# A state-space scan on one core: the inputs of every second unit come from ScalarE and TensorE, and most products with C run on GpSimd

## What is computed

```python
xz = einsum('bld,ed->ble', x, W_in);  xp, z = split(xz, 2)
xc = silu(conv_b + causal_conv(xp, conv_w))             # 512 channels
dbc = einsum('ble,fe->blf', xc, W_x)                    # dt | B (16) | C (16)
delta = softplus(einsum('blr,er->ble', dt, W_dt) + b_dt)
dA  = exp(delta[..., None] * A)                         # 512 channels x 16 states
dBx = delta[..., None] * Bm[:, :, None, :] * xc[..., None]
h_t = dA_t * h_{t-1} + dBx_t                            # scan over 256 tokens
y = einsum('bles,bls->ble', hs, Cm) + xc * Dp
y = y * silu(z);  x = layernorm(x + einsum('ble,de->bld', y, W_out))
# then attention and experts: x = layernorm(x + ffn(x))
```

## Time and profile before

| | us |
|---|---|
| median of 3 runs | 837.95 (837.55 to 838.26) |
| the profiled execution | 834.06 |
| its span, first to last instruction | 832.3 |
| VectorE busy from 70 to 283 us, the scan | 205.84 of 213 |
| GpSimd busy there | 189.78 |
| TensorE busy there | 173.34 |
| ScalarE busy there | 128.25 |

### The profile page before, as it was taken

The page is one execution under the profiler, slowest core; times in us unless marked ns, Lnnn a source line. Parts: engine busy times, 40 slices in busy tenths (PEclk is TensorE's granted clock), DMA queues, the critical chain, the costliest instruction groups (busy, mean ns, idle before and its releaser), DMA issues.

```text
span 832.3 us, 12019 instructions
## 1 busy us (share of the span) xinstructions
PE 753.3 (91%) x3991; PEld 566.9 (68%) x4000; DVE 611.8 (74%) x1243; ACT 452.8 (54%) x957; POOL 327.2 (39%) x183
## 2 busy tenths in 40 slices
PE   6985787788868999999999999998899999999996
PEld 2431233334434588898889898997777889898986
DVE  2688999999998877766884877577657373737376
ACT  3696656667546267755772766476544151515151
POOL 9007999898877832111110121112315030303030
PEclk9996999999999999999999999998989999999999
DMA  8000000000000200100000011011305552525201
GB/s 292 26 1 1 0 1 0 0 0 1 0 1 0 102 1 26 52 26 27 27 26 26 25 38 38 2 39 58 96 1 124 151 150 72 150 70 153 68 0 50
DMA packets 14458, 39.98 MB, mean 48 GB/s; under 512 B 2368, under 2 KB 3904, under 8 KB 14288
## 3 DMA queue, kind: packets, MB, share of 16 engines
q1 hardware_dynamic: 14416, 39.46, 15.5%
HBM read 38.34 MB, written 1.11 MB: 47 GB/s over the span
## 4 chain that ended last, share of the span: by engine, by line
PE 52%; DVE 18%; issue 14%; ACT 11%; POOL 3%; DMA 1%; DVEq 0%; SPq 0%; ACTq 0%; POOLq 0%
PE ps L872 13%; PE ps L874 12%; PE ps L873 12%; PE ps L439 6%; DVE m_ring L749 4%; POOL m_ring L326 2%; ACT a_p L1148 2%; PE ps L370 2%; PE ps L994 2%; DVE m_ring L754 2%; ACT a_vh L1140 2%; PE ps L397 2%; DVE a_p L1248 2%; DVE e_aw L1733 1%; PE ps L443 1%
## 5 line engine op out<-in xcount | busy, mean ns | idle before, releaser
L326 POOL TENSOR_TENSOR m_ring<-m_du,m_b_sb 128x1024 f32<-128x1024 f32 x64 | 149.6, 2358 | 66.9 <-DVE m_du L722 46.3
L749 DVE TENSOR_TENSOR_SCAN m_ring<-ps,m_ring 128x1024 f32<-128x1024 f32 x64 | 145.5, 2283 | 4.6 <-POOL m_ring L326 2.8
L950 POOL TENSOR_TENSOR a_wl<-raw,a_wh 128x1024 fp32r<-128x1024 f32 x16 | 40.0, 2498 | 236.3 <-ACT a_wh L1136 236.3
L439 PE MATMUL ps<-m_ring,ident 128*128 128x512 f32 x256 | 128.8, 618 | 0.1
L1464 POOL TENSOR_TENSOR e_wl<-raw,e_wh 128x512 fp32r<-128x512 f32 (+1 forms) x55 | 58.2, 1067 | 138.8 <-ACT e_wh L1575 74.7
L618 ACT ACTIVATE ps<-m_delta,m_negA 128x510 f32<-128x510 f32 x128 | 82.7, 682 | 6.2 <-DVE m_ring L749 4.2
L439 PEld LDWEIGHTS ps<-m_ring,ident 128*128 128x128 f32 x256 | 50.6, 198 | 44.0 <-issue 41.3
L872 PE MATMUL ps<-a_rowsh,e_wh 128*128 128x512 f32 x200 | 79.6, 398 | 0.7 <-DVE e_aw L1725 0.7
L873 PE MATMUL ps<-a_rowsl,e_wh 128*128 128x512 f32 x200 | 78.9, 395 | 0.0
L874 PE MATMUL ps<-a_rowsh,e_wl 128*128 128x512 f32 x200 | 78.8, 394 | 0.0
L569 ACT ACTIVATE m_b_sb<-ps 128x512 f32<-128x512 f32 x64 | 38.0, 594 | 64.3 <-PE ps L383 61.3
(11 more groups left out here) (202 smaller groups left out, 2067.7 us busy)
## 6 DMA issues: line engine op xcount, KB each, us to landing
raw<-in_expert_w SPq DMA_DIRECT2D x30, 384.0 KB, 3.5
raw<-in_attn_w SPq DMA_DIRECT2D x20, 512.0 KB, 3.3
e_wb<-wt SPq DMA_DIRECT2D x20, 256.0 KB, 4.7
e_wb<-wt SPq DMA_DIRECT2D x4, 448.0 KB, 6.3
e_wb<-wt SPq DMA_DIRECT2D x4, 384.0 KB, 4.5
e_wb<-wt SPq DMA_DIRECT2D x4, 320.0 KB, 4.5
m_first<-in_xT SPq DMA_DIRECT2D x2, 512.0 KB, 5.2
x<-in_x_tok SPq DMA_DIRECT2D x1, 1024.0 KB, 10.6
```

Of the source, the lines that this page charges most:

```text
L326: nc.gpsimd.tensor_tensor(split(slot(n)), du[:, pair_of(ph):pair_of(ph) + 2, halves(ph)], b_sb[:, n % B_BUFS:n % B_BUFS + 1, :].to_broadca ...
L439: nc.tensor.matmul(ps[:, Y_BANK + c, :], ident[:, :], slot(n)[:, c * HALF:(c + 1) * HALF], start=False, stop=False, skip_group_check=True) ...
L749: nc.vector.tensor_tensor_scan(slot(n), dA_of(n), slot(n), 0.0, ALU.mult, ALU.add).then_inc(scan_done, 1)
L950: nc.gpsimd.tensor_tensor(w[1][:, j, :], raw[:, j, :], w[0][:, j, :].bitcast(F32), ALU.subtract).then_inc(w_done, 1)
```

## The change

Units are now handled in pairs, an even one and an odd one.

- **Even units** get their input from GpSimd as before (`unit_in`), but the spread B comes by DMA: rows B and C (fp32) are written to DRAM once, and SyncE loads each row into all 128 partitions (`load_b`), three buffers.
- **Odd units** get their input from ScalarE: `du` is turned once for each chunk and half so that tokens lie on partitions (`turn_du`, `take_du`); B is turned too (`turn_b`, `take_b`), so that it is a scale for each partition; four activations of 128x256 make the product (`product`), and TensorE turns it back into PSUM with eight transposes (`turn_in`), where the scan reads it.
- **Decays**: those of even units stay in PSUM (one buffer of two banks), those of odd units go to SBUF (`decay_of`, two buffers). The other two banks hold the turned input of the odd unit.
- **Products with C**: VectorE makes 25 of the 64, those for which `by_vector` holds, with C spread by TensorE; GpSimd makes 39, with C spread by DMA (`load_c`), three buffers. `broadcast_b`, `copy_b` and `copy_c` are gone.
- Sums into y are added two units later, all in one order, and `pack`, the statistics and the rows of the norm move by some units.

```diff
-B_BUFS = 4
-B_AHEAD = 5
-BY_POOL = UNITS // 4 - 1
+B_BUFS = C_BUFS = 3
...
+TURN_AT = (4, 6, 18, 20, 22, 24)
 
 
 OUT_AT = (36, 44, 52, 56)
 
...
+    DA_BANK, IN_BANK, Y_BANK, TURN_BANK, C_BANK = 4, 6, 2, 0, 1
+
+    def decay_of(n):
+        if n % 2 == 0:
+            return banks(ps, DA_BANK, 2)
+        k = n // 2 % 2
+        if n < UNITS // 2:
+            return wh[:, k * UNIT:(k + 1) * UNIT]
+        return wl[:, (2 + k) * UNIT:(3 + k) * UNIT]
+
+    def du_T(half, i):
+
+        at = (2 - 2 * half) * UNIT + i * E_IN
+        return wl[:, at:at + E_IN]
+
+    PROD_MOVES = UNITS // 2 + 4
+
+    def prod_of(n, i):
+
+
+        k = n // 2 % 2
+        if n < PROD_MOVES:
+            at = (2 + k) * UNIT + i * 2 * P
+            return wh[:, at:at + 2 * P]
+        return delta[:, 2 * k + i // 2, i % 2 * 2 * P:(i % 2 + 1) * 2 * P]
 
...
-        return n - min((n + 3) // 4, BY_POOL)
+        return n % NS % 3 == 1 or n % NS == NS - 1 or n == UNITS - 2
+
+    def vector_below(n):
+        return sum(by_vector(m) for m in range(n))
+
+    def pool_below(n):
+        return n - vector_below(n)
 
...
+        def load_b(n):
+            k = n // 2
+            if k >= B_BUFS:
+                sp.wait_ge(dbx_ready, k - B_BUFS + 1)
+            sp.dma_start(b_sb[:, k % B_BUFS, :], bc_dram[n % NS:n % NS + 1, halves(phase(n))].to_broadcast([P, HALF])
+                         ).then_inc(ld_b[k % B_BUFS], 16)
+
+        def load_c(n):
+            k = pool_below(n)
+            if k >= C_BUFS:
+                sp.wait_ge(hcp_ready, k - C_BUFS + 1)
+            row = NS + n % NS
+            sp.dma_start(c_sb[:, k % C_BUFS, :], bc_dram[row:row + 1, halves(phase(n))].to_broadcast([P, HALF])
+                         ).then_inc(ld_c[k % C_BUFS], 16)
+
+        sp.wait_ge(rows_ready, 1)
+        sp.dma_start(bc_dram, bc_rows).then_inc(rows_stored, 16)
+        sp.wait_ge(rows_stored, 16)
+        load_b(0)
+        load_b(2)
+        load_c(0)
+        for n in range(0, UNITS, 2):
+            if n + 4 < UNITS:
+                load_b(n + 4)
+            for m in (n + 1, n + 2):
+                if m < UNITS and not by_vector(m):
+                    load_c(m)
+
...
-        for n in range(UNITS):
+        for n in range(0, UNITS, 2):
             unit_in(n)
-            if n >= 3 and by_pool(n - 3):
-                times_c(n - 3)
-
+            for m in (n - 3, n - 2):
+                if m >= 0 and not by_vector(m):
+                    times_c(m)
...
+        pool.wait_ge(prod_ready, UNITS // 2)
         for j in range(GH):
             pool.wait_ge(wh_done, j + 1)
+            if j >= 2:
+                pool.wait_ge(scan_done, UNITS - 6 + 2 * j)
...
         def broadcast_c(n):
-            if n and by_pool(n - 1):
-                pe.wait_ge(c_sb_ready, (n - 1) // 4 + 1)
-            nc.tensor.matmul(ps[:, C_BANK, :], sel[:, NS + n % NS, :], bcp[:, halves(phase(n))],
+            if n > 1:
+                pe.wait_ge(hc_ready, vector_below(n))
+            nc.tensor.matmul(ps[:, C_BANK, :], sel[:, n % NS, :], bcp[:, halves(phase(n))],
                              start=True, stop=True).then_inc(c_ready, 1)
+
+        def turn_b():
+
+            for i in range(TT):
+                mm = nc.tensor.transpose(ps[:, TURN_BANK, i * NS:(i + 1) * NS], bc_rows[0:NS, i * P:(i + 1) * P],
+                                         ident[0:NS, 0:NS])
+            mm.then_inc(turn_ready, 1)
+
+        def turn_du(k):
+
+            half, c = k // EC, k % EC
+            pe.wait_ge(turn_free, k + 1)
+            pe.wait_ge(du_ready, c + 1)
+            for i in range(TT // 2):
+                mm = nc.tensor.transpose(ps[:, TURN_BANK, i * P:(i + 1) * P],
+                                         du[:, c, (half * TT // 2 + i) * P:(half * TT // 2 + i + 1) * P], ident[:])
+            mm.then_inc(turn_ready, 1)
+
+        def turn_in(n):
+
+            pe.wait_ge(prod_ready, n // 2 + 1)
+            if n == 1:
+                pe.wait_ge(pair_free, 3 * EC)
+            else:
+                pe.wait_ge(scan_done, n - 1)
+            for c in range(2):
+                for i in range(TT // 2):
+                    mm = nc.tensor.transpose(ps[:, IN_BANK + c, i * P:(i + 1) * P], prod_of(n, i)[:, c * P:(c + 1) * P],
+                                             ident[:])
+            mm.then_inc(in_ready, 1)
 
...
+        def sum_unit(n):
             if n % NS == 0:
                 start_y(phase(n))
-            for back in (1, 2):
-                if n >= back and by_pool(n - back):
-                    pe.wait_ge(hcp_ready, (n - back) // 4 + 1)
-                    sum_y(n - back, back - 1)
-
-        for n in range(UNITS):
-            step(n)
-            if n == UNITS - 4:
-                pe.wait_ge(b_sb_ready, UNITS)
+            if by_vector(n):
+                pe.wait_ge(hc_ready, vector_below(n + 1))
+            else:
+                pe.wait_ge(hcp_ready, pool_below(n + 1))
+            for c in range(2):
+                sum_y(n, c)
+
+        for n in range(UNITS + 2):
+            if n in TURN_AT:
+                turn_du(2 + TURN_AT.index(n))
+            if n - 2 in vector_units[:-1]:
+                broadcast_c(vector_units[vector_units.index(n - 2) + 1])
+            if n == UNITS - 2:
+                pe.wait_ge(o_free, N_OUT)
                 rows.turn(pe, 0, 0)
-            if n == UNITS - 3:
+            if n == UNITS:
                 pe.wait_ge(scan_done, UNITS - 1)
                 rows.turn(pe, 0, 1)
-                pe.wait_ge(o_free, N_OUT)
                 first_parts(5)
+            if n >= 2:
+                sum_unit(n - 2)
+            if n % 2 and n + 2 < UNITS:
+                turn_in(n + 2)
+            if n - 1 in OUT_AT:
+                out_pair(OUT_AT.index(n - 1))
...
+        def take_b():
+            act.wait_ge(turn_ready, 1)
+            nc.scalar.activation(b_T.rearrange("p i s -> p (i s)"), ps[:, TURN_BANK, 0:TT * NS], ACT.Copy
+                                 ).then_inc(turn_free, 1)
+
+        def take_du(k):
+
+            half, c = k // EC, k % EC
+            act.wait_ge(turn_ready, k + 2)
+            if k == 0:
+                act.wait_ge(rows_stored, 16)
+            at = (2 - 2 * half) * UNIT
+            out = wl[:, at:at + 2 * UNIT].rearrange("p (i e) -> p i e", i=TT // 2)[:, :, c * P:(c + 1) * P]
+            nc.scalar.activation(out, ps[:, TURN_BANK, :].rearrange("p (i e) -> p i e", i=TT // 2), ACT.Copy
+                                 ).then_inc(turn_free, 1)
+
+        def product(n):
+
+            ph = phase(n)
             if n >= 4:
-                act.wait_ge(hcp_ready, n // 4)
-            nc.scalar.activation(c_sb, ps[:, C_BANK, :], ACT.Copy).then_inc(c_sb_ready, 1)
+                act.wait_ge(in_ready, n // 2 - 1)
+            if n % NS == 1:
+                act.wait_ge(turn_free, 1 + EC * (ph // 2) + pair_of(ph) + 2)
+            for i in range(TT // 2):
+                tile = ph // 2 * (TT // 2) + i
+                mm = nc.scalar.activation(prod_of(n, i), du_T(ph // 2, i)[:, pair_of(ph) * P:(pair_of(ph) + 2) * P],
+                                          ACT.Copy, scale=b_T[:, tile, n % NS:n % NS + 1])
+            mm.then_inc(prod_ready, 1)
 
...
         act.wait_ge(a_ready, 1)
-        act.wait_ge(dA_zeroed, 1)
-        for n in range(UNITS):
+        act.wait_ge(dA_zeroed, 2)
+        for n in range(0, UNITS, 2):
             decay(n)
-            if n >= 2 and by_pool(n - 2):
-                copy_c(n - 2)
-            if n - B_AHEAD + 1 in OUT_AT:
-                take_out(OUT_AT.index(n - B_AHEAD + 1))
-                copy_b(n + 1)
-            if n + 2 < UNITS and n - B_AHEAD + 2 not in OUT_AT:
-                copy_b(n + 2)
+            decay(n + 1)
+            if n + 3 < UNITS:
+                product(n + 3)
+            if n - 2 in TURN_AT:
+                take_du(2 + TURN_AT.index(n - 2))
+            if n - 4 in OUT_AT:
+                take_out(OUT_AT.index(n - 4))
             if n in PACK_AFTER:
                 pack(PACK_AFTER.index(n))
             if n == ROOTS_AFTER:
                 roots(0)
-            if n in SCALE_AFTER:
-                scale_row(SCALE_AFTER.index(n))
+            for i in range(TT // 2):
+                if n == SCALE_AFTER[i]:
+                    scale_row(i)
         act.wait_ge(keep["ld_ln1"], 16)
-        act.wait_ge(dbx_ready, UNITS)
+        act.wait_ge(dbx_ready, UNITS // 2)
...
         def scan(n):
             dve.wait_ge(dA_ready, n + 1)
-            dve.wait_ge(dbx_ready, n + 1)
-            nc.vector.tensor_tensor_scan(slot(n), dA_of(n), slot(n), 0.0, ALU.mult, ALU.add).then_inc(scan_done, 1)
+            if n % 2:
+                dve.wait_ge(in_ready, n // 2 + 1)
+                if n >= RING:
+                    dve.wait_ge(summed, 2 * (n - RING + 1))
+                unit_in = banks(ps, IN_BANK, 2)
+            else:
+                dve.wait_ge(dbx_ready, n // 2 + 1)
```

(2 more changed lines are left out.)

138 lines of the change are left out of this document (64 added, 74 removed).

## The result

The changed kernel takes **812.76 us** at the median (809.37 to 816.08 in four runs), against 837.75 for the kernel before on the same chip: a ratio of 0.9703 (95% interval 0.9669 to 0.9736), 25 us faster. The prediction was 815, range 804 to 832. The profiled execution of the changed kernel took 816.08 us, the longest of its four; they fall into two pairs, 815.65 and 816.08 at a mean granted clock of 0.968, and 809.37 and 809.88 at 0.978 and 0.982. The profiled execution of the kernel before (834.06, clock 0.974) is shorter than each of its four times here (836.95 to 838.26). So the two profiles, set side by side, show less than the whole gain.

The account below looks back on a forecast made before the run. VectorE's own instructions in the scan stage were taken to bound the kernel. 834.06 - 26.9 - 7.0 + 7.8 + 1.5 + 0.5 + 1.0 = 811.0, plus 3.9 for the median gives 815 us, range 804 to 832.

Parts of the forecast that it names:

- Products leaving VectorE, -26.9: Scan stage: VectorE makes 25 products with C instead of 49, so 24 at 1.12 us, 26.9 us, go.
- GpSimd 97% full: Scan stage: GpSimd's 18 instructions take 41.6 us of a 42.9 us phase; its work stays hidden with 1.3 us to spare.
- Scans of both forms, ScalarE's product, the loads: Scan stage: odd scans cost the same 2.19 us; a 128x256 activation takes 0.49 us; loads landing in 4.7 us stay hidden.
- The waits of before, -7.0: Scan stage: VectorE's earlier waits for spread C, GpSimd's input and decays inside the stage go, 7.0 us.
- The new wait behind output pairs, +7.8: Scan stage: VectorE waits for turned inputs queued behind four output pairs on TensorE, 2.7 us twice and 1.2 twice.
- the layout by hand: Scan stage: one phase laid out with the paces, timing GpSimd's products, TensorE's sums and turns against VectorE's need.
- The clock at the start, +1.5: Scan stage: low TensorE clock (0.50 from 70 to 76 us) makes some turns late by one or two us; 1.5 put.
- The stage, 190: From first scan to last product with C: 190 us instead of 213.
- Start +0.5, end +1.0: ScalarE's work before the first scan adds 0.5 us; TensorE's norm turns ahead of the last two sums add 1.0.
- A wait at most odd units: Scan stage: GpSimd and TensorE pass delays to turns, 0.5 us at 32 odd units, 16 us more: 829; chance 0.20.
- GpSimd falling behind: Scan stage: GpSimd's products wait 1.5 us each for DMA-loaded rows, 58 us: 868; chance 0.04 slower, 0.02 the same.
- The rule of the Trainium skill on transposes: TensorE in the stage: transposes don't count as clock activity like matmuls, pushing towards a low-clock slowdown; that case's chance 0.06.

Follow-up runs that it names:

- experiment 6: The changed kernel with four more products with C on GpSimd (43 instead of 39) and four fewer on VectorE (21 instead of 25): 816.19 us.
- experiment 3: The changed kernel with six added fp32 matmuls of 128x512, results unused, around TensorE's first turns at the start of the scan: 811.45 us.

## Why the prediction was right, and where it was not

- **Products leaving VectorE, -26.9.** 49 became 25 at 1.20 us each. Put back alone they brought 22.4 us of VectorE's work and 19.8 of stage. As terms of the same sum: VectorE's work fell by 25.3, which is 26.9 less the 2.6 by which short operations grew, and 1.0 more, half of it scans that are shorter by 8 ns (2.275 us for 2.283), the rest less overlap lost than the sum took off. That GpSimd's load would hold up VectorE's short operations was in no term.
- **GpSimd 97% full.** 71 operations at 2.36 us, but busy for 90% (170.7 of 189.5 us): it idled 18.9 us, nearly all of it waiting for scans. That it had no room for more was right (experiment 6), though not because it was full: what came too late was single products.
- **Scans of both forms, ScalarE's product, the loads.** 2.28 us for both, 0.494 for a taken 0.49, and 3.5 (C) and 4.0 us (B) to landing for a bound of 4.7. None of them made VectorE wait.
- **The waits of before, -7.0.** The sum took them all away. In their place are 1.9 us of small waits, which no term held.
- **The new wait behind output pairs, +7.8.** The mechanism was right, the size was not: 2.53 and 1.36 us at the first two, none and 0.53 with the last two, 4.4 in all for 2.7 + 2.7 + 1.2 + 1.2. The first was met in each part (pair, two sums, turn). At the second VectorE had one more product with C of its own to make meanwhile, which the layout by hand had left out.
- **The clock at the start, +1.5.** 2.7 us, in one piece at unit 5. The idle time is 4.4 + 2.7 + 1.9 = 9.0 for a predicted 9.3: that these errors (-3.4, +1.2, +1.9) cancel is luck.
- **The stage, 190.** It is 189.5. But the prediction's own terms for it, 212.8 - 26.9 - 7.0 + 7.8 + 1.5, give 188.2; its 190 counts the start and the end (+1.5) in, which lie outside the stage.
- **Start +0.5, end +1.0.** Measured -0.8 and +0.8. du was finished 0.9 us earlier than before, so GpSimd and ScalarE could begin sooner. Together they are 1.5 less than predicted, and the stage's gain is 1.3 less (23.3 for 24.6): the sum of -23.1 against a measured -23.3 is as close as it is because the two cancel.
- **The rivals.** A wait at most odd units did not come: there was none of over 0.3 us at 28 of the 32. GpSimd falling behind needs more work than the change gave it, and no load was late. The mean clock of the stage was 0.96. The rule of the Trainium skill on transposes, which would have brought it down, is not borne out at this mix of turns and matmuls; where the clock did fall (70 to 80 us, and 100 to 105 in experiment 3) TensorE had been idle for part of the time ahead.
- **A slip that changes nothing.** In the paragraph on GpSimd, 24 x 1.1 is 26.4, not 27.
- **The median.** The 3.9 us stood for a profiled execution of the kernel before that was shorter than its median. Taken from the same start, 837.95 - 23.3 = 814.7, and the median is 812.76, 1.9 lower, which is within the spread of its executions. The profiled execution was 816.08 for a predicted 811.0, by the 5.4 us of the routing stretch (clock 0.86 for 0.92), which the sum did not hold; with the 90.1 us of before it would have had 810.7.

## What to carry to other kernels

When one engine sets the pace and another takes over its work, lay out the second one's order of work for each period before moving, and not only its sum: with 71 instructions it was in time, with 75 its products came late in three places, at 92% busy. Count in also what it does to the first engine: beside a GpSimd operation some of VectorE's short operations took up to 2.40 us instead of 0.17, which cost 4.4 us here. Where an input is made in a short window in the order of an in-order queue, long optional work (here the output pairs) should be cut to pieces that fit the slack and placed behind the urgent step; that gave back 3.8 us. And compare medians before trusting the difference of two profiles in an untouched stage: 5.4 us seemed lost there, and between the medians nothing was.

## What the runs showed of the hardware that was not expected

- A VectorE operation with two operands in SBUF, and a TENSOR_SCALAR with one, ended no earlier than the GpSimd operation beside it: 0.17 us became up to 2.40, once 3.71 over two GpSimd operations; 25 operations of 128x16 took 776 ns on average, and 150 ns with one operand in PSUM. A BATCH_NORM_STATS2 with one SBUF input was not held up (0.40 us).
- The same instructions took 90.0 to 95.7 us in the routing stretch, with mean granted clocks of 0.92 down to 0.86. Four executions of the same kernel on one chip had 809.4 to 816.1 us, the two shorter ones at the higher clock.
- Keeping TensorE busy ahead of a dip can move it and save next to nothing (70 to 76 us, then 100 to 105 us; stage 189.5 to 189.0).
- The decays written to SBUF by ScalarE take 706 ns, those to PSUM 678.
